# A GAT and mixture-of-experts kernel: the wait in the middle of each group of row gathers is put on the sums of the tile before instead of on the landing of the group's first half

## What is computed

```python
hh = (x @ W).reshape(n, H, D)
s_src = jnp.einsum('nhd,hd->nh', hh, a_src)
s_dst = jnp.einsum('nhd,hd->nh', hh, a_dst)
scores = jax.nn.leaky_relu(s_src[src] + s_dst[dst], negative_slope=0.2)
m = jax.ops.segment_max(scores, dst, num_segments=n)
e = jnp.exp(scores - m[dst])
denom = jax.ops.segment_sum(e, dst, num_segments=n)
alpha = e / denom[dst]
msgs = hh[src] * alpha[:, :, None]
out = jax.ops.segment_sum(msgs, dst, num_segments=n).reshape(n, H * D)
out = out + x
...
return jax.nn.elu(out)
```

## Time and profile before

| | us |
|---|---|
| median of 3 runs | 3319.01 |
| lowest and highest run | 3306.84 and 3321.35 |
| the profiled execution's own time | 3321.35 |
| its span, first to last instruction | 3319.6 |
| POOL's first and last gather of `stage3` (starts) | 177.2 and 2687.7 |
| busy: PE, DVE, ACT, POOL | 1870.8, 1679.0, 1036.6, 1857.2 |
| mean granted TensorE clock, as a share of full speed | 0.775 |

### The profile page before, as it was taken

How to read it: one execution, slowest core, us unless ns; L and a number is a source line. 1 busy time by engine, 2 the same in 40 slices (tenths; PEclk the granted TensorE clock), 3 DMA queues, 4 the chain that set the end, 5 groups by cost and what they waited for, 6 DMA issues and landing times. The chain is left out here.

```text
span 3319.6 us, 43546 instructions
## 1 busy us (share of the span) xinstructions
PE 1870.8 (56%) x9190; PEld 1519.2 (46%) x9191; DVE 1679.0 (51%) x3940; ACT 1036.6 (31%) x2031; POOL 1857.2 (56%) x1944
## 2 busy tenths in 40 slices
PE   6255555555545445555455445444455436999975
PEld 5144434434334334433334334333344326898964
DVE  7555555555555554555555555555555532333346
ACT  4232332323323232232323323233232312333342
POOL 2456666666666666656666666666666633555520
PEclk9677777777777777777777777777777767999987
DMA  5443343443433434343443434434344336333343
GB/s 187 117 118 107 108 123 106 122 122 105 122 107 118 117 112 118 108 121 105 123 122 106 123 105 123 122 105 122 108 119 118 112 91 218 101 102 100 101 161 116
DMA packets 179756, 393.55 MB, mean 119 GB/s; under 512 B 52144, under 2 KB 100576, under 8 KB 173448
## 3 DMA queue, kind: packets, MB, share of 16 engines
q0 software_dynamic: 93984, 273.52, 28.8%
q1 hardware_dynamic: 69512, 105.33, 10.2%
q10 hardware_dynamic: 16224, 14.30, 1.5%
HBM read 356.52 MB, written 36.47 MB: 118 GB/s over the span
## 5 line engine op out<-in xcount | busy, mean ns | idle before, releaser
L1265 POOL DMA_INDIRECT gat<-table,idx x1632 | 1547.8, 948 | 976.1 <-DMA gat<-table,idx 525.3
L1362 PE MATMUL ps_sum<-msg,hot 128*128 128x264 f32 x3332 | 1165.9, 525 | 1207.6 <-DVE msg L1409 1101.8
L1362 PEld LDWEIGHTS ps_sum<-msg,hot 128*128 128x128 f32 x3332 | 878.3, 270 | 1434.7 <-issue 1222.8
L1398 DVE TENSOR_TENSOR both<-gat,ps_own 128x144 f32<-128x144 f32 x196 | 58.0, 296 | 831.6 <-DMA gat<-table,idx 745.6
L1409 DVE TENSOR_TENSOR msg<-gat,ps_weight 128x2304 f32<-128x2304 f32 x196 | 472.5, 2411 | 5.4 <-issue 5.4
L1321 ACT ACTIVATE ps_weight<-score 128x72 f32<-128x72 f32 x196 | 45.2, 231 | 680.1 <-issue 413.4
L1406 DVE TENSOR_TENSOR hot<-ps_own,rel 128x1152 f32<-128x1152 f32 x196 | 251.0, 1281 | 0.0
L2089 PE MATMUL ps_ht<-xT,w_t 128*128 128x128 f32 x1712 | 215.2, 279 | 3.0 <-DVE w_t L2122 1.7
L2013 POOL DMA_INDIRECT chosen<-o_sb,put_at x105 | 123.9, 1180 | 151.1 <-DMA chosen<-o_sb,put_at 129.1
L2089 PEld LDWEIGHTS ps_ht<-xT,w_t 128*128 128x128 f32 x1712 | 201.4, 193 | 11.0 <-DVE w_t L2122 6.0
L2098 PE MATMUL ps_o<-w_sb,hidT 128*128 x840 | 198.7, 379 | 0.0
(11 more groups left out here) (397 smaller groups left out, 2099.6 us busy)
## 6 DMA issues: line engine op xcount, KB each, us to landing
dst_row<-dst_half SPq DMA_DIRECT2D x49, 1088.0 KB
gat<-table,idx POOLq DMA_INDIRECT x1666
b_t<-in_L_ffn_b_dram ACTq DMA_DIRECT2D x107, 128.0 KB
w_sb<-in_L_ffn_w_dram SPq DMA_DIRECT2D x6, 2048.0 KB, 12.4
listing<-list_f SPq DMA_DIRECT2D x736, 0.5 KB
back<-chosen SPq DMA_DIRECT2D x5, 1792.0 KB, 7.7
table<-rows SPq DMA_DIRECT2D x49, 128.0 KB, 1.7
y_rows<-y SPq DMA_DIRECT2D x49, 128.0 KB
```

The lines of the kernel that those rows point to most:

```text
L1265: pool.indirect_dma_start(gat[:, GSTART[g] + k, :], None, table, bass.IndirectOffsetOnAxis(ap=idx[g][:, k:k + 1], axis=0)).then_inc(landed ...
L1362: last = pe.matmul(ps_sum[:, 0:SUM], hot[:, m, k, :], msg[:, m, k, :], start=(g == 0 and k == 0), stop=(g == NG - 1 and k == n - 1))
```

## The change

One line changes. Ahead of the second half of group g of tile t, POOL waited until the gathers of the group's first half had landed. It now waits until TensorE has summed the same group of the tile before. The order of the gathers, their buffers and all other waits stay.

```diff
@@ -1260,7 +1260,7 @@
                     pool.sem_inc(pool_turn, 1)
                     for k in range(GROUPS[g]):
                         if k == GROUPS[g] // 2:
-                            pool.wait_ge(landed[g], t * (16 * GROUPS[g]) + 16 * (GROUPS[g] // 2))
+                            pool.wait_ge(sum_done, (t - 1) * NG + g + 1)
                             pool.sem_inc(pool_turn, 1)
                         pool.indirect_dma_start(gat[:, GSTART[g] + k, :], None, table,
                                                 bass.IndirectOffsetOnAxis(ap=idx[g][:, k:k + 1], axis=0)).then_inc(landed[g], 16)
```

## The result

The changed kernel took 3360.45 us (median of 4 runs, 3359.12 to 3363.24), the kernel before 3316.80 beside it (4 runs, 3306.84 to 3321.35): a ratio of 1.014, interval 1.0115 to 1.0165. It is slower by 44 us; forecast was 3142, faster.

A forecast was written before the change was run, and what follows sets the result against it. POOL's gathers and waits were taken to pace the tile at 52.3 us, then a ring over SP at 49.0. From 3321.35, taking off 149 (ring), 17 (first tiles) and 13 (last tile) gave 3142 us, range 3050 to 3240.

The forecast's parts named there:

- POOL paces the tile: Main loop: 34 gathers of 1.25 us plus 4 longer gaps on POOL make the tile's 52.3 us.
- The new wait costs nothing: POOL's mid-group wait in the loop: the sums lie three groups back, some 39 us, so it is met at once.
- Can the gathers run without a pause?: POOL's gather queue: the opening's 36 gathers without landing waits show it can; from this alone the tile falls to 42.5 us.
- the chain of DVE, ACT and PE: Tile without gather waits: 35.3 us, or 39.2 if the head's 3.86 us wait for PE doubles, 10 us below 49.
- the ring over SP: List copy, list writes, `dst_row` load, `rows`, next copy: closes at 49.0 us a tile, so the gain is 3.3 us; chance 0.80.
- Term 2: SP, first list write to `dst_row` issue: 30.5 us mean, none of it a wait for POOL.
- Term 3: `dst_row` issue to ACT's start of `rows`: 6.9 us, taken between 6.6 and 7.3.
- Term 4: ACT's `rows` to the end of DVE's next list copy: 10.6 us with no further gap, now 12.0.
- POOL's pace: Rival in the loop: the ring shrinks below 42.5 us, all 468 us come back, 2853 us; chance 0.09.
- Transfer bound: Rival on the gathers: their transfers limit at 1.54 us each, so no change, 3321 us; chance 0.05.
- The gathers crowd out SP's load: Rival at the `dst_row` load: it takes 11.6 us, double its quiet 5.8, so slower, 3354 us; chance 0.06.
- The even split of the engines' time: DMA engines during the `dst_row` load: shared evenly with an always full gather queue, giving 3354 us.

The follow-up runs named there:

- s1_depth: Kernel before with its mid-group wait now for the landing of the whole group before, in a set with late signals: 3914.42 us, ratio 1.1701.
- r6_both: Kernel before plus the new wait ahead of the old one, on another chip with late look-up signals: 3319.68 us, ratio 1.001.
- t3_after: The changed kernel run again in the fifth set, on a fourth chip with signals on time: 2849.04 us, ratio 0.8452 of the kernel before.
- s3_spread: Kernel before without landing wait, each gather preceded by a waited-for clearing of 64 floats per partition, 1.93 us from gather to gather: 3999.46 us, ratio 1.1953.
- e1_both: Kernel before plus the new wait ahead of the old one, in the first set, signals on time: 3375.55 us, ratio 0.9998.

## Why the prediction was wrong, point by point

**POOL paces the tile: right.** With the wait gone and signals on time the tile falls to 42.6 us.

**The new wait costs nothing: right in both conditions as long as the old one stands beside it** (0.9998 and 1.001), and with signals on time the changed kernel equals the one without a wait (0.8452 and 0.8449). With late signals the reckoning that the sums lie "three groups back, some 39 us" fails: POOL runs ahead by up to a tile and meets the wait unfulfilled in 125 places.

**"Can the gathers run without a pause?" is the step that failed.** The gathers can: their landings stayed prompt even in rows of 16 and 18 (`s1_depth`). The question was put to POOL's queue alone. In the condition of the traces, rows of gathers 1.25 us apart hold back TensorE's signals and slow SP's sequencer, the longer the row the worse: with rows of 8 and 9 hardly one of the sums' signals is late (1 of 121 before, 0 of 127 in `r6_both`), with 17, 9, 4 and 4 about half are, by 6.6 us in the mean, and with 18 and 16 by 11.2. The old wait, which read as 468 us lost, let signals through in time for DVE. Taking it out cost 16.6%; the wait put in its place gives back all but 1.3%. Its rows are shorter, 17, 9, 4 and 4, because it too breaks them, though later. My opening rows showed only a landing, and no TensorE signal was needed there in time.

**The sum's term that was mis-sized is the chain of DVE, ACT and PE at the tile's head.** I let the wait for the sums double, from 3.86 to 7.7 us. It was 14.2, of which 8.6 is the late signal; the matmuls' own 5.7 us, at a granted clock of 0.66, lie within the 7.7. Without any mid-group wait this is plain, since POOL then stands 1043.3 us at messages that wait behind the division; in the changed kernel the ring over SP, with the same late signals in it, has the same length, and no run took the two apart.

**The ring over SP.** Its four stretches over 45 tiles, mean us, each forecast beside what the changed kernel showed in either condition (worked out from the starts and ends of the rows' instructions):

| | forecast | late signals | on time |
|---|---|---|---|
| `list_f` copy to first list write | 1.0 | 3.8 | 1.0 |
| first list write to `dst_row` issue | 30.5 | 27.7 | 20.1 |
| `dst_row` issue to `rows` | 6.9 | 10.9 | 9.8 |
| `rows` to the next copy | 10.6 | 10.4 | 11.8 |
| sum | 49.0 | 52.7 | 42.6 |

- Term 2 was wrong in kind: "None of it is a wait for POOL" was true, yet POOL made it long. With signals on time the same instructions take 20.1 us. With the forecast's terms 3 and 4 the ring then needs 1.0 + 20.1 + 6.9 + 10.6 = 38.6, under POOL's 42.5, and doesn't close; the rest up to 42.6 is waiting.
- Term 3: the load itself lands as forecast; see below. ACT's wait in the changed kernel, 5.8 us in the tile shown, was for TensorE's look-up signal. The row of 10.2 us in the earlier trace rows hints at it already: what ended its wait is "remote", and not a DMA as in the first load of that group. I read it as a slow landing. It was none; the row behind this list has more.
- Term 4 was right in the late condition, 10.4 for 10.6, with no gap.

Term 3 was misread already in the trace of before. What ended ACT's waits at this line there, by the same kind of view as the earlier trace rows:

```profile
L1277 ACT ACTIVATE hotT<-dst_row,neg_id x48: 3909/3910/3922, 187.6 to 2629.6; 128x4352 bf16<-128x4352 int16 x48
...
  remote: 10.9, 11
  PE ps_look L1348: 4.6, 2
```

None is a DMA. In the signal events of the row of 10.2 us, TensorE's look-ups end at 2047.84, their signal comes at 2054.47, and ACT starts at 2054.59; in that of 7.3 us the three times are 1527.46, 1532.59 and 1532.71. So neither row says how long the load takes.

**The rivals.** POOL's pace, 2853 us, with 0.09, is what happens with signals on time: 2849 there, if from a before of 3373; the condition I set for it, term 2 under 24, was met by 20.1. But I saw no reason for term 2 to fall, so the 0.09 was no insight, only a bound kept open. "Transfer bound" fell. "The gathers crowd out SP's load", 3354 us, gave the measured time in the slower condition (3360) for the wrong reason. The changed kernel's DMA queues, in two stretches of 2 us behind the `dst_row` issue at 1555.75 (q0 carries the gathers, q1 what SP issues, here the load above all; packets, MB, share of the 16 engines' time):

```profile
DMA packets 52, 0.45 MB, mean 226 GB/s; under 512 B 0, under 2 KB 0, under 8 KB 0
...
q1 hardware_dynamic: 52, 0.45, 72.1%
```

```profile
q0 software_dynamic: 145, 0.43, 63.1%
q1 hardware_dynamic: 63, 0.05, 6.8%
```

The first is 1558 to 1560, the second 1562 to 1564: the load has the engines to itself in the first and is nearly over in the second, 6.3 us after its issue. If anything, it held up the gathers. The Trainium skill, "DMA: Bandwidth & Descriptors", section "Queues, rings and completion order", says that each DMA engine takes the queues that have work in turn, packet by packet. The even split of the engines' time was my own reading of that, and the first stretch, where the gather queue moved nothing, does not bear it out.

**Sign.** I gave slower 0.06, and that for another cause. No row of the trace of before states the condition, but two carried its mark and so did the signal events: 28 us for 16 small writes, 2.25 us ended by "remote", and the look-ups' signals late by 3.5 us in 154 of 156 cases. There they cost little, because DVE needed hardly one of them earlier (its look-up line L1394 waited 3.6 us in the whole kernel).

**Open.** Why dense gathers hold back TensorE's signals and SP's instructions, and what puts a chip into the one condition or the other, no run tells; both have been seen on one chip.

One rival is untested and has a sign in its favour: the recording of the profile itself. Every timed run was a profiled one, and the traces of the two conditions differ in how many semaphore events they hold, though all hold the same DMA packets to within 4 of 179,768. For the changed kernel's 43,456 instructions it is 19,420 events in the trace after the change and 45,003 in `t3_after`. The seven with signals on time hold 44,807 to 46,082 events. Twelve of the thirteen with late signals or of a set that has them hold 17,507 to 19,923; the thirteenth is `s3_spread`, whose signals are on time, with 40,258. In the trace of before, 5.0 events per us are on record in the loop, against 13.6 in that of `e1_both`, and in the first 100 us, ahead of the gathers, both have 14.6. So whatever delays the signals also goes with lost event records, and both fade when the gathers are spread. Whether the unprofiled kernel has late signals at all is not shown, nor therefore whether the change makes that one slower.

Where between 1.25 and 1.93 us of spacing the effect ends is open too. Freeing POOL for a part of the gap (waiting for a landing two gathers earlier) was not tried, since a count of landings doesn't tell which gathers they were. Of the versions run in both conditions, none beats the kernel before in both: the changed kernel is 0.845 or 1.012 to 1.014 of it, the one without a wait 0.845 or 1.166, the one with two landing waits 0.911 or 1.055, and the one with both waits 1.000 or 1.001. Of the first three the changed kernel is at least as good as the others in either.

## What to carry to other kernels

A pause on the engine that paces a kernel may be doing something for the others: before you count it as gain, ask what each other engine's signals and issues look like inside the dense stretches that remain, and what they look like in the gap. A wait that the profile ends with "remote", or with work that was over long before, and a row of small DMA issues that takes 1.5 times as long as elsewhere, are marks of the same thing. And measure a change that packs DMA issues closer on more than one chip and occasion, with the kernel before beside it each time, and if you can once without the profiler.

## What the runs showed of the hardware that was not expected

- The same kernel without mid-group waits took 2854 us on one occasion and 3890 on another, the kernels before beside them 3378 and 3339. The condition in which the old kernel is the faster by 1% is the one in which the one without mid-group waits is slower by over a third.
- In it, TensorE's signals arrive late in long rows of gathers 1.25 us apart (the sums' signals that are late by 6.6 us in the mean with rows of up to 17, by 11.2 with rows of 16 and 18), and SP needs 26 to 29 us for 16 address loads and writes in place of 18.3. DVE's and ACT's signals are not affected, and the gathers' landings came in time for the wait of `s1_depth`. With gathers 1.93 us apart none of it is seen.
- The traces of that condition hold 17,507 to 19,923 semaphore events, those of the other 44,807 to 46,082, and the one with gathers 1.93 us apart 40,258.
- In the condition with signals on time a mid-group gap is longer, 3.05 us over the 192 of `e1_both` against 2.74 in the trace of before; 192 x (3.05 - 0.30) = 528 us, and 3373 - 528 = 2845 is the changed kernel's 2849.
- A clearing of 16 floats per partition between two gathers is free on POOL (0.13 us, spacing 1.26 instead of 1.25); one that is waited for adds 0.68 us.
